# A 64-wide attention whose rotation takes one projection instead of two, with VectorE writing the sine products across blocks of 32 partitions

## The chip, the core and the metric

The kernel runs on one core of one Trainium2 chip. The metric is the device time of one execution in microseconds. Three runs of the kernel before gave 2931.18, 2931.95 and 2934.36 us. TensorE (PE) has two clock levels, 1.2 and 2.4 GHz; the profile states the granted clock as a share of the higher one. VectorE is DVE, ScalarE is ACT, GpSimd is POOL and SyncE is SP in the views.

## What is computed

The reference is a small hybrid network of two layers; the change touches only its first attention, `L0_attn_a`. Input x is 2 batches of 1024 tokens with 128 channels, layer-normalized before it comes in.

```python
NQ, NKV, HD, RANK = 16, 4, 64, 8          # 16 query heads share 4 key/value heads
def _lora_proj(x, W, A, Bm):
    return x @ W.T + x @ A.T @ Bm.T * LORA_SCALE
def _rope(x, cos_h, sin_h):
    x1, x2 = (x[..., ::2], x[..., 1::2])
    return jnp.concatenate([x1 * cos_h - x2 * sin_h, x1 * sin_h + x2 * cos_h], axis=-1)
q, k = _rope(q, cos_h, sin_h), _rope(k, cos_h, sin_h)
attn = jax.nn.softmax(jnp.einsum('bhqd,bhkd->bhqk', q, k) * ATTN_SCALE, axis=-1)
out = jnp.einsum('bhqk,bhkd->bhqd', attn, v)
return _lora_proj(out, Wo, qA..., oA, oB)
```

There is no mask: each of 16 heads x 2 batches has 1024 x 1024 scores.

## The kernel before, in words

`attention_l0a` loads the weights of the first key/value group and the tables, then `wide_heads` runs the whole attention in one block in which every engine has its own written-out order. The work is cut into `WINDOWS` = 8 windows (group g = w // 2, batch b = w % 2), and each window into `STEPS` = 32 steps; a step is one head's 128 query rows against all 1024 keys. So there are 256 steps, and in each:

- TensorE (L906 on) multiplies the scores of step s (L917, L918: four matmuls against the high and low parts of k), turns eight 128 x 128 blocks of finished rows of step t = s - 10 (L932), in every second step multiplies two such pieces with V (L944), and last does one of the jobs that `wide_jobs` placed in this step (`spare`).
- VectorE takes the row maximum of the scores (L1025), copies half of the turned blocks (L1031), takes the reciprocal of the sums of step s - 1 (L1037), writes low parts (`low`, L993) and reads the job's result (`read`).
- ScalarE copies the other half of the turned blocks (L967), takes the exponential with the row sum (L972), once in eight steps copies the head output (L977), divides the row of step s - 2 if `on_act` says so (L981), and writes high parts (`high`, L956 and L958).
- GpSimd adds cosine and sine products (L1056) and divides the other rows (L1059).

The turned blocks of a set of eight rows may start only when all eight rows are divided (L926, L927): transposes of a step s with s % 8 == 2 wait for the row of step s - 3. Scores wait for the exponential two steps back (L915), transposes for both copies of the step before (L930). GpSimd and VectorE go through their lists strictly in order, so a wait holds all that stands behind it.

A rotation unit ("rope") is one (window, u) with u from 0 to 5: u 0 and 1 are the two halves of k's 1024 tokens for a window, u 2 to 5 are two heads of q for one half each. Before the change, one unit is two jobs: f = 0 projects x with the columns in rotation order, f = 1 with the columns of each pair of halves swapped. VectorE multiplies the first by the cosine table into `t_cos`, the second by the signed sine table into `t_sin` (L1012), two buffers each. GpSimd adds them. ScalarE writes the rounded value once whole into `t_hi` and once into the stack (`Kh`, or the upper or lower 64 partitions of `Qw`), and VectorE writes the remainder, value minus rounded value, into the low stack (`Kl`, or the other 64 partitions of `Qw`). Scores of a window use the units made in the window before. The lead (step -1) does the first window's low-rank product and its units 0 to 2. Other jobs are "lora" (low-rank update of the weights of a group, L881 to L887), "value" (V of a window, L894) and "out" (the output projection, L902). All jobs share bank 7 of PSUM except those of the lead.

## Time and profile before

| | before |
|---|---|
| median of 3 runs | 2931.95 us |
| profiled execution, its time / its span | 2932.3 / 2930.6 us |
| PE matmul busy | 2285.7 us, 78% of the span |
| DVE / ACT / POOL busy | 1552.0 / 1456.3 / 903.7 us (53 / 50 / 31%) |
| mean granted TensorE clock | 0.876 |
| this attention | about 43 to 957 us of the span |

The shares hold for the whole program; the attention above takes the first third of it. In the page's line of 40 slices of 73 us, TensorE is at 9 tenths or more and at the full clock in slices 2 to 13, VectorE at 7, ScalarE at 6 to 7, GpSimd at 7. One reads such a profile by stretches: first which engine is full in the stretch, then its order of time, then what it waits for. Matmul ends are modelled, so the distance between starts says more than a single duration.

### The profile page before, as it was taken

The page shows a single profiled execution, that of the slowest core. Times are in us where ns is not written, and L with a number is a line of the kernel's source. Part 1 is how long each engine was busy: PE and PEld are TensorE (multiplying, and loading weights), DVE is VectorE, ACT ScalarE, POOL GpSimd, SP SyncE. Part 2 cuts the span into 40 slices and gives each one's busy share as a digit, 9 for nine tenths or more (in the row PEclk, how much of TensorE's full clock was granted, in tenths as well). Part 3 has the DMA queues.
Part 4 walks back from the last instruction along what each step waited for, and adds up shares of the span by engine and source line. Part 5 has one row for each costly group of instructions (what it writes and reads, how often), then busy time and mean ns, then how long its engine had stood idle before and what let it go on. Part 6 is the DMA issues. An engine that isn't in the chain of part 4 may idle for free. (4 is left out here: it accounts for less than half of the span.)

```text
span 2930.6 us, 38170 instructions
## 1 busy us (share of the span) xinstructions
PE 2285.7 (78%) x13956; PEld 1360.2 (46%) x13966; DVE 1552.0 (53%) x3280; ACT 1456.3 (50%) x2248; POOL 903.7 (31%) x512
## 2 busy tenths in 40 slices
PE   3999999999999339499428485899869515999788
PEld 2566666666665218333317343344347313344366
DVE  3767777777764351411351363677523395677323
ACT  2666666666675422488432244355633312555532
POOL 3776776777774102422201303100010122000100
PEclk9999999999999559699659798799979755999889
DMA  2000000000000300321300121211000002210000
GB/s 67 8 1 1 3 8 1 3 8 1 3 1 1 119 0 1 84 57 33 119 0 1 51 69 40 63 43 34 2 15 22 0 0 55 64 41 18 1 22 29
DMA packets 41593, 79.77 MB, mean 27 GB/s; under 512 B 11448, under 2 KB 20200, under 8 KB 37256
## 3 DMA queue, kind: packets, MB, share of 16 engines
q1 hardware_dynamic: 41416, 77.43, 9.7%
q8 instruction: 108, 1.77, 0.2%
q14 instruction: 69, 0.57, 0.1%
HBM read 63.03 MB, written 13.63 MB: 26 GB/s over the span
## 5 line engine op out<-in xcount | busy, mean ns | idle before, releaser
L648 ACT ACTIVATE probs<-psum_banks 128x1024 f32<-128x1024 f32 (+3 forms) x608 | 474.2, 826 | 360.3 <-PE psum_banks L513 253.1
L1059 POOL TENSOR_SCALAR l0a_rows<-l0a_rows,l0a_rinv 128x1024 f32<-128x1024 f32 x192 | 562.3, 2935 | 251.8 <-DVE l0a_rinv L1037 251.5
L721 DVE TENSOR_REDUCE neg_max<-psum_banks 128x1 f32<-128x512 f32 (+3 forms) x672 | 398.8, 658 | 201.1 <-PE psum_banks L546 149.5
L1025 DVE TENSOR_REDUCE l0a_nmax<-psum_banks 128x1 f32<-128x1024 f32 x256 | 312.9, 1222 | 208.1 <-PE psum_banks L918 207.4
L508 PE MATMUL psum_banks<-q_stack,k_stack 75*128 75x512 bf16 (+7 forms) x1216 | 322.7, 344 | 74.7 <-ACT probs L648 25.9
L972 ACT ACTIVATE l0a_rows<-psum_banks,l0a_nmax 128x1024 f32<-128x1024 f32 x256 | 285.9, 1117 | 79.8 <-DVE l0a_nmax L1025 77.5
L542 PE MATMUL psum_banks<-k_stack,q_stack 72*128 72x128 bf16 (+3 forms) x1024 | 250.7, 328 | 77.7 <-DMA q_stack<-q_parts 66.1
L932 PE MATMUL psum_banks<-packed,l0a_rows 128*128 128x128 f32 x2048 | 268.9, 274 | 7.8 <-POOL l0a_rows L1059 6.3
L932 PEld LDWEIGHTS psum_banks<-packed,l0a_rows 128*128 128x128 f32 x2048 | 238.8, 141 | 52.5 <-POOL l0a_rows L1059 11.5
L917 PE MATMUL psum_banks<-l0a_kh,l0a_qw 128*128 128x512 f32 x512 | 256.5, 501 | 6.2 <-DVE l0a_qw L993 5.9
L530 PE MATMUL psum_banks<-probs,v_ones 128*32 128x512 f32 (+3 forms) x2432 | 242.5, 514 | 7.5 <-ACT o_sum L617 6.5
L334 POOL TENSOR_SCALAR x_norm<-x_res,ln_mv,ln_rstd 128x128 f32<-128x128 f32 x128 | 101.4, 806 | 442.9 <-DVE ln_rstd L312 442.9
L508 PEld LDWEIGHTS psum_banks<-q_stack,k_stack 75*128 75x128 bf16 (+1 forms) x1216 | 105.5, 100 | 252.5 <-ACT probs L648 102.8
L918 PE MATMUL psum_banks<-l0a_kl,l0a_qw 128*128 128x512 f32 x512 | 204.9, 400 | 0.0
L334 POOL TENSOR_SCALAR x_norm<-l1f_y,ln_mv,ln_rstd 128x128 f32<-128x128 f32 x32 | 24.9, 792 | 540.1 <-DVE ln_rstd L312 540.1
L542 PEld LDWEIGHTS psum_banks<-k_stack,q_stack 72*128 72x128 bf16 x1024 | 95.7, 105 | 201.6 <-DVE neg_max L721 90.3
L1555 DVE SCALAR_TENSOR_TENSOR l1f_y<-psum_banks,rt_g,l1f_y 128x128 f32<-128x128 f32 x256 | 72.2, 345 | 168.3 <-PE psum_banks L1533 168.1
L917 PEld LDWEIGHTS psum_banks<-l0a_kh,l0a_qw 128*128 128x128 f32 x512 | 97.4, 190 | 134.9 <-issue 79.2
L967 ACT ACTIVATE x_norm<-psum_banks 128x512 f32<-128x512 f32 x128 | 75.9, 593 | 138.7 <-PE psum_banks L932 138.5
L1523 PE MATMUL psum_banks<-x_norm_t,l1f_w 128*128 128x512 f32 x256 | 117.2, 618 | 23.3 <-PEq L69 14.1
L513 PE MATMUL psum_banks<-tri_k,ident_b 128*128 128x128 bf16 (+1 forms) x566 | 127.9, 243 | 0.0
L944 PE MATMUL psum_banks<-x_norm,l0a_v 128*64 128x512 f32 x512 | 124.0, 604 | 3.7 <-ACT l0a_ot L977 3.7
(259 smaller groups left out, 3596.5 us busy)
## 6 DMA issues: line engine op xcount, KB each, us to landing
q_stack<-q_parts SPq DMA_DIRECT2D x96, 192.0 KB
k_stack<-k_parts SPq DMA_DIRECT2D x72, 192.0 KB
qkv<-in_l0f_w SPq DMA_DIRECT2D x6, 1024.0 KB, 5.5
q_parts<-parts SPq DMA_DIRECT2D x24, 256.0 KB
k_parts<-parts SPq DMA_DIRECT2D x24, 256.0 KB
l1f_w<-in_l1f_w SPq DMA_DIRECT2D x20, 256.0 KB, 2.9
moe_w<-in_l0f_w SPq DMA_DIRECT2D x2, 1024.0 KB, 5.5
packed<-in_packed SPq DMA_DIRECT2D x1, 1875.5 KB
```

The costliest lines, as they stand in the source:

```text
L508: m = pe.matmul(PS[:, bank, c0:HALF], S.Kst[0:rows_of_stack, slot(g, i), kt * P:(kt + 1) * P], S.Qst[0:rows_of_stack, slot(g, i), side * H ...
L513: m = pe.matmul(PS[:, bank, c0:c1], S.ident_b[:], S.tri_k[:, 0:c1 - c0], start=False, stop=True, skip_group_check=True)
L530: m = pe.matmul(PS[32 * i:32 * (i + 1), 7, c0:HALF], S.Vx[:, NT * b + kt, h0 + i, :], S.Pt[:, U % PBUFS, i, c0:HALF], start=kt == 0, stop= ...
L542: return pe.matmul(bank[:, at:at + k1 - k0], S.Qst[0:72, slot(g, i), jq * P:(jq + 1) * P], S.Kst[0:72, slot(g, i), k0:k1], start=first, st ...
L648: act.activation(S.Pt[:, U % PBUFS, 2 * half:2 * half + 2, c0:HALF], PS[:, bank:bank + 2, c0:HALF], ACT.Exp).then_inc(exp_done, 1)
L721: dve.tensor_reduce(out, scores, AX, ALU.max, negate=True).then_inc(job_read, 1)
L917: pe.matmul(scores(s)[:, c0:c0 + HALF], q, R.Kh[:, b, c0:c0 + HALF], start=True, stop=False)
L918: m = pe.matmul(scores(s)[:, c0:c0 + HALF], q, R.Kl[:, b, c0:c0 + HALF], start=False, stop=True)
L932: m = pe.transpose(PS[:, 4 + a, jj * P:(jj + 1) * P], R.Pr[:, (NT * ps + 2 * jj + a) % RING, kt * P:(kt + 1) * P], S.ident[:])
L972: act.activation(R.Pr[:, s % RING, :], scores(s), ACT.Exp, bias=R.nmax4[:, s % 4:s % 4 + 1], accum_out=R.rsum4[:, s % 4:s % 4 + 1]).then_i ...
L1025: dve.tensor_reduce(R.nmax4[:, s % 4:s % 4 + 1], scores(s), AX, ALU.max, negate=True).then_inc(max_done, 1)
L1059: pool.tensor_scalar(R.Pr[:, s % RING, :], R.Pr[:, s % RING, :], R.rinv4[:, s % 4:s % 4 + 1], None, ALU.mult).then_inc(pool_normed, 1)
```

## The change

One projection per unit. The swapped columns are gone from the weights: 448 columns per group instead of 896, and the sine table's signs are exchanged. VectorE multiplies the projection by the cosine as before, and then writes the sine product in four parts: part i reads partitions 32i to 32i + 31 of the projection and of the table, and writes to the neighbouring block of 32. Parts 0 and 1 come in the job's step, parts 2 and 3 at the job's place in the next step, after its reciprocal. The scale of q is in these multiplies. GpSimd's sum comes one step after the job, and now GpSimd also writes the low parts, three steps after it, subtracting the high part in its stack; VectorE's `low` and ScalarE's whole copy `t_hi` are gone. ScalarE writes the high parts three steps after the job. Rows divided on ScalarE are those with s % 8 in (1, 4, 6) instead of s % 4 == 1, that is 96 instead of 64 of 256. `wide_jobs` places the units at steps 1, 5, 9, 11, 19 and 21 of a window, those of window 1 at 9, 11, 13, 15, 17 and 19 of window 0. VectorE's cosine multiply of a unit waits until the high and low parts of the unit two before are done.

```diff
-    rope = [[("rope", w, u, f) for u in range(6) for f in range(2)] for w in range(WINDOWS)]
-    total, at = WINDOWS * STEPS, {-1: [("lora", 0, 0), ("lora", 0, 1)] + rope[0][:6]}
...
+    rope = [[("rope", w, u) for u in range(6)] for w in range(WINDOWS)]
+    total, at = WINDOWS * STEPS, {-1: [("lora", 0, 0)] + rope[0][:3]}
...
+            jobs = {1: rope[0][3], 3: rope[0][4], 5: ("value", 0), 7: rope[0][5], 21: ("value", 1), 23: ("lora", 0, 1)}
+            jobs.update(zip(range(9, 21, 2), rope[1]))
         else:
...
+            jobs = {15: ("out", w - 1, 0), 17: ("out", w - 1, 1)}
+            if not last:
+                jobs[13] = ("value", w + 1)
+                jobs.update(zip((1, 5, 9, 11, 19, 21), rope[w + 1]))
+        if w % 2 and g:
+            jobs[3] = ("lora", g, 1)
+        if w % 2 == 0 and g + 1 < NKV:
+            jobs[31] = ("lora", g + 1, 0)
...
+        sums_at.setdefault(s + 1 if s >= 0 else s, []).append(n)
+        highs_at.setdefault(s + 3 if s >= 0 else s, []).append(n)
+        lows_at.setdefault(s + 3 if s >= 0 else s, []).append(n)
...
     def on_act(s):
 
-        return s % 4 == 1
+        return s % 8 in (1, 4, 6)
...
                     if part == 0:
-                        m = pe.matmul(PS[:, bank, :], R.la[:, 0, :], R.lb[:, 0:512], start=True, stop=True)
-                    elif part == 1:
-                        pe.matmul(PS[:, bank, 0:256], R.la[:, 1, :], R.lb[:, 512:768], start=True, stop=True)
-                        m = pe.matmul(PS[:, bank, 256:384], R.la[:, 2, :], R.lb[:, 768:896], start=True, stop=True)
+                        for i, (c0, c1) in enumerate(((0, 256), (256, 384), (384, 448))):
+                            m = pe.matmul(PS[:, bank, c0:c1], R.la[:, i, :], R.lb[:, c0:c1], start=True, stop=True)
...
             def high(u):
-                scale, parts = targets(u)
                 act.wait_ge(summed, u + 1)
-                act.activation(R.t_hi[:, u % 2, :], R.t_cos[:, u % 2, :], ACT.Copy, scale=scale).then_inc(hi_done, 1)
-                for ch, hi, lo in parts:
-                    ins = act.activation(hi, R.t_cos[ch, u % 2, :], ACT.Copy, scale=scale)
-                ins.then_inc(copied, 1)
+                for rows, hi, lo in targets(u):
+                    ins = act.activation(hi, R.t_cos[rows, u % 2, :], ACT.Copy)
+                ins.then_inc(hi_done, 1)
...
-            def low(u):
-                scale, parts = targets(u)
-                dve.wait_ge(hi_done, u + 1)
-                dve.wait_ge(copied, u + 1)
-                for ch, hi, lo in parts:
-                    ins = dve.scalar_tensor_tensor(lo, R.t_cos[ch, u % 2, :], scale, R.t_hi[ch, u % 2, :].bitcast(F32),
-                                                   ALU.mult, ALU.subtract)
-                ins.then_inc(lo_done, 1)
+            def turn_part(job, blocks):
+
+                u = unit_no[job[1:]]
+                for i in blocks:
+                    src, to = slice(32 * i, 32 * i + 32), slice(32 * (i ^ 1), 32 * (i ^ 1) + 32)
+                    ins = dve.scalar_tensor_tensor(R.t_sin[to, u % 2, :], PS[src, bank_of(job), :], scale_of(job),
+                                                   R.sinT[src, job[2] % 2 * HALF:(job[2] % 2 + 1) * HALF], ALU.mult, ALU.mult)
+                return ins
...
                     if u >= 2:
-                        dve.wait_ge(lo_done, u - 1)
-                    table, to = ((R.cosT, R.t_cos), (R.sinT, R.t_sin))[f]
-                    ins = dve.tensor_tensor(to[:, u % 2, :], PS[:, bank, :], table[:, k % 2 * HALF:(k % 2 + 1) * HALF], ALU.mult)
+                        dve.wait_ge(hi_done, u - 1)
+                        dve.wait_ge(lo_done, low_parts(u - 2))
+                    dve.scalar_tensor_tensor(R.t_cos[:, u % 2, :], PS[:, bank, :], scale_of(job),
+                                             R.cosT[:, job[2] % 2 * HALF:(job[2] % 2 + 1) * HALF], ALU.mult, ALU.mult)
+                    turn_part(job, (0, 1))
+                    return
...
+                for job in at.get(s - 1, ()) if s > 0 else ():
+                    if job[0] == "rope":
+                        turn_part(job, (2, 3)).then_inc(job_read, 1)
...
+            def low(u):
+
+                pool.wait_ge(hi_done, u + 1)
+                for rows, hi, lo in targets(u):
+                    for own in (sums, rows_divided, lows):
+                        if own.n:
+                            own.wait()
+                    lows.link(pool.tensor_tensor(lo, R.t_cos[rows, u % 2, :], hi.bitcast(F32), ALU.subtract))
+
             for s in range(-1, total):
                 for u in sums_at.get(s, ()):
...
+                    total_of(u)
+                    if s < 0:
+                        low(u)
+                for u in lows_at.get(s, ()) if s >= 0 else ():
+                    low(u)
                 if s >= 0 and not on_act(s):
                     pool.wait_ge(inv_done, s + 1)
```

## Rows read from the trace of the kernel before

**Rows 1.** Stretches: us, busy us of PE, PEld, DVE, ACT, POOL, clock, DMA.

```profile
61.00:94.00 33.00, 26.61 (x91) 18.29 (x92) 23.29 (x33) 19.04 (x32) 24.57 (x10) 0.81 0.00 1
...
153.00:920.00 767.00, 759.89 (x4154) 487.25 (x4155) 549.32 (x848) 523.05 (x868) 547.48 (x208) 1.00 0.01 3
```

**Rows 2.** TensorE in order of time, two steps with a job: start, us, instruction.

```profile
302.47 0.50 PE L917 MATMUL psum_banks<-l0a_kh,l0a_qw 128*128 128x512 f32 x1
...
309.02 0.50 PE L917 MATMUL psum_banks<-l0a_kh,l0a_qw 128*128 128x512 f32 x1
```

**Rows 3.** TensorE in order of time, two steps without a job.

```profile
865.08 0.50 PE L917 MATMUL psum_banks<-l0a_kh,l0a_qw 128*128 128x512 f32 x1
...
870.74 0.50 PE L917 MATMUL psum_banks<-l0a_kh,l0a_qw 128*128 128x512 f32 x1
```

**Rows 4.** Waits from 94 to 920 us: total us, times, longest.

```profile
PE psum_banks L932 <- POOL l0a_rows L1059: 4.1, 10, 1.0
...
PE psum_banks L944 <- ACT l0a_ot L977: 3.7, 8, 0.5
```

**Rows 5.** Groups of VectorE, 42 to 960 us: busy us, mean ns; idle before.

```profile
L1025 DVE TENSOR_REDUCE l0a_nmax<-psum_banks 128x1 f32<-128x1024 f32 x256 | 312.9, 1222 | 208.1 <-PE psum_banks L918 207.4
...
L1031 DVE COPY x_norm<-psum_banks 128x512 f32<-128x512 f32 x128 | 87.3, 682 | 11.7 <-PE psum_banks L932 11.2
...
L1037 DVE RECIPROCAL l0a_rinv<-l0a_rsum 128x1 f32<-128x1 f32 x256 | 39.3, 153 | 0.2
...
L993 DVE SCALAR_TENSOR_TENSOR l0a_qw<-l0a_tc,l0a_ts 64x512 fp32r<-64x512 f32 x64 | 66.5, 1039 | 5.2 <-ACT l0a_qw L958 3.9
```

**Rows 6.** VectorE in order of time: a pair on changing partitions, then two neighbours.

```profile
59.82 1.39 DVE L993 SCALAR_TENSOR_TENSOR l0a_qw<-l0a_tc,l0a_ts 64x512 fp32r<-64x512 f32 x2 [1.38 <-ACT l0a_qw L958]
...
98.63 0.69 DVE L1012 TENSOR_TENSOR l0a_tc<-psum_banks,l0a_cos 128x512 f32<-128x512 f32 x1
...
99.23 1.21 DVE L1025 TENSOR_REDUCE l0a_nmax<-psum_banks 128x1 f32<-128x1024 f32 x1
```

**Rows 7.** Groups of ScalarE, 42 to 960 us, same columns.

```profile
L972 ACT ACTIVATE l0a_rows<-psum_banks,l0a_nmax 128x1024 f32<-128x1024 f32 x256 | 285.9, 1117 | 79.8 <-DVE l0a_nmax L1025 77.5
...
L972 ACT ACTIVATION_READ_ACCUMULATOR l0a_rows<-psum_banks,l0a_nmax 128x1 f32 x256 | 49.9, 195 | 0.0
...
L967 ACT ACTIVATE x_norm<-psum_banks 128x512 f32<-128x512 f32 x128 | 75.9, 593 | 138.7 <-PE psum_banks L932 138.5
...
L981 ACT ACTIVATE l0a_rows<-l0a_rows,l0a_rinv 128x1024 f32<-128x1024 f32 x64 | 73.2, 1143 | 0.0
...
L958 ACT ACTIVATE l0a_qw<-l0a_tc 64x512 fp32r<-64x512 f32 x64 | 39.9, 623 | 0.4
```

**Rows 8.** Single lines: instruction, count, ns min/median/max, first and last start.

```profile
L1056 POOL TENSOR_TENSOR l0a_tc<-l0a_tc,l0a_ts x48: 1263/1284/1777, 51.9 to 810.2; 128x512 f32<-128x512 f32 x48
...
L1059 POOL TENSOR_SCALAR l0a_rows<-l0a_rows,l0a_rinv x192: 2836/2845/3343, 66.7 to 927.3; 128x1024 f32<-128x1024 f32 x192
...
L993 DVE SCALAR_TENSOR_TENSOR l0a_qw<-l0a_tc,l0a_ts x64: 684/689/1762, 59.8 to 820.5; 64x512 fp32r<-64x512 f32 x64
```

**Rows 9.** All engines in order of time, around the lead.

```profile
45.42 0.69 DVE L1005 SCALAR_TENSOR_TENSOR l0a_w<-psum_banks,l0a_w 128x512 f32<-128x512 f32 x1 [21.94 <-PE psum_banks L881]
...
61.36 0.77 PE L917 MATMUL psum_banks<-l0a_kh,l0a_qw 128*128 128x512 f32 x1 [5.94 <-DVE l0a_qw L993]
```

**Rows 10.** TensorE in order of time, window 0, idle before in brackets.

```profile
79.25 1.31 PE L890 MATMUL psum_banks<-x_norm_t,l0a_w 128*128 128x512 f32 x2 [3.58 <-DVE l0a_tc L1012]
...
94.47 1.91 PE L932 MATMUL psum_banks<-packed,l0a_rows 128*128 128x128 f32 x8
...
152.85 1.09 PE L932 MATMUL psum_banks<-packed,l0a_rows 128*128 128x128 f32 x8 [1.03 <-POOL l0a_rows L1059]
```

**Rows 11.** DMA from 20 to 60 us: the queue (packets, MB), one transfer (KB).

```profile
q1 hardware_dynamic: 640, 1.69, 13.9%
...
l0a_w<-in_l0a_w SPq DMA_DIRECT2D x1, 448.0 KB
```

More of the change, by code:

```diff
@@ L808, in wide_heads @@
     lead = len(at[-1])
-    units = [job[1:3] for job in order if job[0] == "rope" and job[3] == 1]
+    units = [job[1:3] for job in order if job[0] == "rope"]
     unit_no = {u: n for n, u in enumerate(units)}
-    done_at = [step_of["rope", *u, 1] for u in units]
+    done_at = [step_of["rope", *u] for u in units]
     sums_at, highs_at, lows_at = {}, {}, {}
     for n, s in enumerate(done_at):
-        sums_at.setdefault(s, []).append(n)
-        highs_at.setdefault(s + 2 if s >= 0 else s, []).append(n)
-        next_use = step_of["rope", *units[n + 2], 0] if n + 2 < len(units) else total
-        lows_at.setdefault(min(s + 4, next_use) if s >= 0 else s, []).append(n)
+        sums_at.setdefault(s + 1 if s >= 0 else s, []).append(n)
+        highs_at.setdefault(s + 3 if s >= 0 else s, []).append(n)
+        lows_at.setdefault(s + 3 if s >= 0 else s, []).append(n)
     def item(s):
@@ L888, in spare @@
                 elif job[0] == "rope":
-                    pe.wait_ge(job_read, number["lora", job[1] // B, 1] + 1)
+                    pe.wait_ge(job_read, number["lora", job[1] // B, 0] + 1)
                     m = pe.matmul(PS[:, bank, :], columns(job), x[:, job[1] % B, job[2] % 2 * HALF:(job[2] % 2 + 1) * HALF],
@@ L893, in spare @@
                     for k in range(NT):
-                        m = pe.matmul(PS[:, bank, k * HD:(k + 1) * HD], x[:, job[1] % B, k * P:(k + 1) * P], R.W[:, 768:832],
+                        m = pe.matmul(PS[:, bank, k * HD:(k + 1) * HD], x[:, job[1] % B, k * P:(k + 1) * P], R.W[:, 384:448],
                                       start=True, stop=True)
@@ L911, in _ @@
                         u = unit_no[s // STEPS, 2 + s % STEPS // NT]
[L912 to L913 removed]
+                        pe.wait_ge(hi_done, u + 1)
+                        pe.wait_ge(lo_done, low_parts(u))
                     if s >= 2:
@@ L1037, in _ @@
                     dve.reciprocal(R.rinv4[:, r % 4:r % 4 + 1], R.rsum4[:, r % 4:r % 4 + 1]).then_inc(inv_done, 1)
-                if s < 0:
-                    for job in at[s]:
-                        if job[0] == "rope" and job[3] == 0 and unit_no[job[1:3]] >= 2:
-                            low(unit_no[job[1:3]] - 2)
-                        read(job)
-                    for u in lows_at[s][-2:]:
-                        low(u)
-                else:
-                    for u in lows_at.get(s, ()):
-                        low(u)
-                    for job in at.get(s, ()):
-                        read(job)
+                for job in at.get(s - 1, ()) if s > 0 else ():
+                    if job[0] == "rope":
+                        turn_part(job, (2, 3)).then_inc(job_read, 1)
@@ L1051, in _, with total_of @@
+                for job in at.get(s, ()):
+                    read(job)
+                    if s < 0 and job[0] == "rope":
+                        turn_part(job, (2, 3)).then_inc(job_read, 1)
         @block.gpsimd
         def _(pool):
+            sums, rows_divided, lows = Chain(pool, summed), Chain(pool, pool_normed), Chain(pool, lo_done)
+            def total_of(u):
+                pool.wait_ge(job_read, number["rope", *units[u]] + 1)
+                sums.mark(pool.tensor_tensor(R.t_cos[:, u % 2, :], R.t_cos[:, u % 2, :], R.t_sin[:, u % 2, :], ALU.add))
@@ L1737, in layouts @@
     half = np.concatenate([np.arange(0, HD, 2), np.arange(1, HD, 2)])
-    swap = np.concatenate([half[HD // 2:], half[:HD // 2]])
     cols = []
     for g in range(NKV):
-        q, k, v = [], [], []
-        for pair in range(2):
-            h0 = g * REP + 2 * pair
-            for order in (half, swap):
-                q += [h0 * HD + order, (h0 + 1) * HD + order]
-        for order in (half, swap):
-            k += [g * HD + order] * 2
-        v = [g * HD + np.arange(HD)] * 2
-        cols.append((np.concatenate(q), np.concatenate(k), np.concatenate(v)))
+        q = [(g * REP + h) * HD + half for h in range(REP)]
+        cols.append((np.concatenate(q), np.concatenate([g * HD + half] * 2), g * HD + np.arange(HD)))
     def per_group(q, k, v):
```

64 lines of the change are left out of this document (25 added, 39 removed).

## The prediction

> **What bounds the kernel now.** I read the stretches first. From 153 to 920 us, where seven of the eight windows of the first attention lie, TensorE is busy 99% of the time at a granted clock of 1.00; VectorE, ScalarE and GpSimd are at 72, 68 and 71% [rows 1]. The reader should see one full engine and three with a quarter left. The second view is TensorE's order of time. Two steps with one rotation job (scores, eight transposes, job, scores, eight transposes, the product with V) take 309.02 - 302.47 = 6.55 us, two without a job 870.74 - 865.08 = 5.66 us [rows 2, 3]. A rotation projection thus costs 0.89 us of the pace. The third view is the waits: TensorE's idle time on GpSimd's divided rows is 4.1 us in 10 places and 3.7 us in 8 on the copy of the head output [rows 4]. So in those windows TensorE's own work is the pace, and what is taken from it counts, as long as no other engine becomes late.
>
> **The sum starts from** the profiled execution, 2932.3 us for a span of 2930.6; 1.7 us lie around it, and it stands 0.35 us above the median of the runs, 2931.95. Nothing outside this stage is edited, so I leave the rest alone.
>
> **TensorE's work.** Each window's 12 projections become 6: 6 x 0.89 = 5.3 us. The low-rank product shrinks from 896 to 448 columns per group. A rotation's 512 columns cost 0.89, so this is 0.78 per group, 0.4 per window: 5.7 us per window. Work for windows 1 to 6 plus their share is removed; window 7 has no rotation job.
>
> **VectorE.** A unit loses one multiply, and its low part (one operation for k, two for q); it gains four sine parts on 32 partitions each. What does one part cost? Two neighbours on the same partitions follow at 99.23 - 98.63 = 0.60 although each lasts 0.69; a pair of L993 that changes partitions halfway took 1.39, so 0.70 each [rows 6]. The parts change partitions every time, so I take 0.70 and keep 0.60 as the low end; the high end is L993's mean beside GpSimd, 1.04 [rows 5]. In the Trainium skill, "VectorE: DVE Perf Modes", section "Two Vector instructions with no wait between them", an instruction whose input or output starts in another group of 32 partitions than its predecessor's begins only once everything earlier is finished; by it every part and the reduce behind it pay the full length.
> A unit then takes cosine 0.7 + 4 x 0.7 = 3.5 us, in two steps, beside 2 x 1.9 for reduce, copy and reciprocal (1.15 + 0.6 + 0.15, [rows 5] less the overlap): 7.3 us against TensorE's 6.55 for the same two steps. One rotation is absorbed; two in neighbouring odd steps, as at 9/11 and 19/21, are not.
> I walk steps 19 to 24 from the start of scores 19, with each engine in its order. TensorE alone would begin transposes 24 at 15.8. VectorE begins reduce 19 at 1.25, runs three rotation blocks (2.1, 1.4, 2.1) and three times 1.9, and reaches reduce 22 at 12.6. The exponential starts 1.26 later, lasts 1.2 with its accumulator, then ScalarE divides row 20 (1.15), writes the high parts of the unit of step 19 (2 x 0.62) and only then copies transposes 23 (0.6) [rows 7]: 18.05. TensorE needs that bank for transposes 24: 2.25 us late (1.2 if parts follow at 0.60). The same pair of jobs, divide and high parts, returns in step 24, and row 23 on GpSimd comes behind row 21, a sum and two low parts: 0.7 us more at step 26. At 9/11 TensorE waits only 0.25 us for a VectorE copy, since the value and output jobs of steps 13 and 15 give slack (eight matmuls with weights of their own, each at a quarter of 0.89: 1.8 us). Before, by the code's step numbers, the high parts met no divide in half of the windows, and a job in nearly every second step gave slack.
> ScalarE in total: 48 full high parts go (48 x 0.62 = 30 us), 32 divides come (32 x 1.14 = 37 us); its share hardly moves, its place does.
>
> **GpSimd.** 32 rows leave (32 x 2.84 = 91 us), 16 + 64 low parts come. Nothing shows a subtract on 64 partitions there; the sum of 128 x 512, 1.28 us [rows 8], is nearest, with the same 512 elements in a partition: 80 x 1.28 = 103 us. Bounds: 0.7 (half, if partitions counted) and 1.8, the longest L1056. In windows 1 to 7 the row before a transposed set of eight (row 6) moves to ScalarE, so row 7 starts at once; I give back the waits on rows, 0.7 us per window (4.1 us in [rows 4], and what follows late behind them), and four times 0.4 = 1.7 in window 7. Against it: without a job in step 3 or 27 the product with V waits for the copy of the head output, about 0.5 us in seven more places, 0.6 per window.
> L1059's times run from 2836 to 3343 ns and L993's from 684 to 1762 [rows 8], the long ones side by side; both go, as VectorE no longer has an operation with two SBUF inputs. In the Trainium skill, "SBUF — State Buffer", section "SBUF: two separate sides", only such operations (or the fast modes) take the port pair that GpSimd uses, so the sine parts should leave its rows at 2.84; the trace agrees, as L1012 reads PSUM and one table and lasts 0.69 beside it [rows 6].
>
> Per window: -5.7 + 2.25 + 0.7 + 0.25 + 0.6 - 0.7 = -2.6; six windows: -15.6. Window 7: -1.7.
>
> **The lead.** Now: low-rank read at 45.42, first scores at 61.36 [rows 9]. After: the shorter product and a single read let the first projection start about 1.5 us earlier, at 45.8; its cosine follows 2.1 later, as now; five operations per unit: units finished at 51.4, 54.9, 58.4. Behind the last: sum 1.28, two high parts 1.25, two low parts 2.6 on GpSimd, with hand-overs 63.7: +2.4. The load moves 448 KB less 224 [rows 11] of 1.69 MB, an eighth of a landing of 6 to 10 us: -0.7 (0 to -1.3).
>
> **Window 0.** Here units follow every two steps from 9 to 19, and VectorE's cosine of unit n waits for the low part of unit n-2 on GpSimd, two steps back. GpSimd has the row, the next unit's sum and that low part ahead: cosine and two parts 2.1, next reduce, copy, reciprocal 1.9, row 2.84, sum 1.28, low 1.3 or 2.6: 9.4 to 10.7 us per two steps where TensorE wants 6.55. Behind VectorE's wait stand the next reduce, and so exponential and scores. I followed this queue by the same prices: the cosines of window 1's units 1 to 5 may start 38.8, 48.4, 58.0, 69.0 and 78.5 us after scores 0, and then rows 18, 19, 21 and 23, a sum and two pairs of low parts bring GpSimd to 97.8, which frees transposes 26. Before, they came at 152.85 - 61.36 = 91.5, having waited 1.03 for GpSimd too [rows 9, 10]: +6.3. In that, the first ten steps gain: first transposes at 30.4 instead of 94.47 - 61.36 = 33.1. Behind it the low-rank job of step 31 is 0.9 shorter.
>
> **Sum:** -15.6 - 1.7 + 2.4 - 0.7 + 6.3 - 0.9 = -10.2: 2932.3 - 10.2 = 2922.1, less 0.35 to stand to the median: about 2922. What is late next is ScalarE's copy in steps 22 to 24, not TensorE.
>
> **Rivals.** *Full relief.* If the parts overlap (0.60) and slack swallows the rest, a window saves 5.7 + 0.7 - 1.0: six give -32; with the lead +1.7, window 0 at +1 and window 7: -31, 2901. For it: the three engines have a quarter free. Against: the walk above, with little freedom in it. *The clock.* In window 0 TensorE would idle a third of the time. Before, the stretch 61 to 94, with an idle of 3.58 us in it, stood at 0.81, so at 1.2 GHz in part [rows 1, 10]. If window 0 falls there for some ten steps (3.2 us of work doubles against a pace of 5.0), it costs 1.4 each, up to 14, central 7: 2929. Against: that stretch was 81% busy with gaps and still mostly at 2.4 GHz. *Slower: dear parts.* If a 32-partition part costs 1.04 like L993 beside GpSimd, each is 0.34 dearer. Six lie ahead of exponential 22 (+2.0), six ahead of step 12 (+1.5 beyond the slack), the two other blocks +0.5: +4.0 per window, +24, window 0's loop +4, the lead +4: 2922 + 32 = 2954. It turns from gain to loss at about 0.1 us per part above my price, 0.80. Against: no second SBUF input. A milder form, GpSimd's low part at 1.8, adds 0.5 x 12 in window 0 and 2 x 0.5 per window: +12, 2934. That the change doesn't do what it says can't be: the projections are gone from the code.
>
> **How the numbers follow.** Forecast 2914 to 2927: 0.42. Full relief: 0.24. Clock, or both small losses, 2927 to 2937: 0.20. Slower by dear parts or low parts: 0.14. The range leaves 0.1 beyond each end: 2899 to 2940. A measurement of this kernel tells 0.2%, 5.9 us, from no change: faster means below 2926.1, slower above 2937.8. Faster: nearly all of the forecast and the relief, 0.63; within: 0.24; slower: 0.13.
>
> **What would show it.** Right: projections 96 instead of 192 records; two neighbouring steps without job at 5.66, with one 6.55; sine parts of 0.69 that follow at 0.70; TensorE waiting on the ScalarE copy once or twice per window by about 2 us; VectorE cosine waiting on GpSimd in window 0; scores 0 near 63. Wrong: TensorE still 99% busy in windows 1 to 6, a granted clock below 1.00 there, GpSimd low parts far from 1.28, window 0 shorter than before.

## The result, and the profile after

The changed kernel takes 2941.93 us (median of 6 runs, 2939.27 to 2945.15) against 2930.86 for the kernel before (6 runs, 2927.70 to 2934.36): ratio 1.0039, 95% interval 1.0026 to 1.0051. It is slower by 11 us, where 2922 was predicted with a range of 2899 to 2940; slower had a chance of 0.13 there. The profiled execution took 2940.4 us for a span of 2938.3.

To see where the time went, I cut the stage at the start of the exponential of each window's first step. All lengths are us from the traces; 0-10, 10-26 and 26-32 are the steps within window 0.

```
              exp 0   w0     w1     w2     w3     w4     w5     w6     w7    | 0-10  10-26  26-32
before        64.7   109.5  109.6  107.7  110.3  108.6  110.3  107.5   95.6  | 31.4   58.3   19.9
changed       65.3   120.3  108.3  109.5  108.3  109.5  108.3  108.3   95.0  | 32.0   69.5   18.8
```

Window 0 is 10.8 us longer, the six steady windows together are only 1.7 shorter, window 7 is 0.6 shorter and the start 0.6 later. That is +9.1; what lies outside this stage gave 1.0 back.

The same two stretches as in [rows 1], now of the changed kernel (columns: stretch, its length, busy us of PE, PEld, DVE, ACT, POOL, granted clock, DMA):

```profile
61.00:94.00 33.00, 22.67 (x65) 14.90 (x66) 24.38 (x36) 17.13 (x26) 21.96 (x12) 0.76 0.00 0
153.00:920.00 767.00, 736.71 (x4102) 477.23 (x4101) 573.18 (x896) 540.36 (x863) 533.51 (x244) 1.00 0.01 2
```

TensorE was busy for 759.89 of 767 us before and now for 736.71. So its work did fall, but nearly all of what was taken away came back as idle time, at the full clock. VectorE rose from 549 to 573 us. TensorE's waits from 94 to 920 us, answering to [rows 4] (what waits, for whom: total us, times, longest):

```profile
PE psum_banks L935 <- ACT x_norm L968: 9.4, 6, 1.6
PE psum_banks L947 <- ACT l0a_ot L978: 7.6, 18, 0.6
PE psum_banks L935 <- DVE x_norm L1034: 7.3, 12, 1.9
PE psum_banks L935 <- POOL l0a_rows L1075: 5.0, 6, 0.8
PE psum_banks L893 <- DVE l0a_ts L994: 3.8, 5, 1.0
PE psum_banks L935 <- DVE l0a_cols L1034: 3.8, 2, 1.9
PE psum_banks L897 <- DVE l0a_ts L994: 3.4, 7, 0.5
```

Before there were two entries above 1.0 us, on GpSimd's rows and the head output. Now every engine holds TensorE somewhere. L994 are the sine parts: the projection (L893) and the value job (L897) wait for them because they free the one spare bank. The prediction had no such wait.

The prices of the single operations came out as forecast (groups over 61 to 920 us; busy us, mean ns | idle before):

```profile
L994 DVE SCALAR_TENSOR_TENSOR l0a_ts<-psum_banks,l0a_sin 32x512 f32<-32x512 f32 x180 | 123.6, 687 | 3.2
L1064 POOL TENSOR_TENSOR l0a_qw<-l0a_tc,l0a_qw 64x512 fp32r<-64x512 f32 x63 | 80.1, 1271 | 11.2 <-POOL l0a_qw L1064 5.2 <-POOL l0a_rows L1075 3.1 <-ACT l0a_qw L959 0.4
```

Four parts in a row took 2.79 us in the lead, 0.70 each. The low part on GpSimd costs 1.27 on 64 partitions.

### The profile page after: what moved, and what is told of

Its sections match the earlier page's. It is cut to its first block and busy times, and to the rows that moved or that the text cites. A ratio compares the mean times of both kernels' runs of the same rounds, so it can differ in the third digit from the quotient of the medians.

```text
span 2938.3 us, 38125 instructions
## 1 busy us (share of the span) xinstructions
PE 2247.8 (77%) x13860; PEld 1344.8 (46%) x13870; DVE 1582.7 (54%) x3340; ACT 1469.2 (50%) x2232; POOL 896.6 (31%) x560
## 3 DMA queue, kind: packets, MB, share of 16 engines
q8 instruction: 107, 1.75, 0.2%
## 5 line engine op out<-in xcount | busy, mean ns | idle before, releaser
L1075 POOL TENSOR_SCALAR l0a_rows<-l0a_rows,l0a_rinv 128x1024 f32<-128x1024 f32 x160 | 454.9, 2845 | 221.6 <-DVE l0a_rinv L1040 218.6
L935 PE MATMUL psum_banks<-packed,l0a_rows 128*128 128x128 f32 x2048 | 272.1, 275 | 27.6 <-ACT x_norm L968 10.1
L920 PE MATMUL psum_banks<-l0a_kh,l0a_qw 128*128 128x512 f32 x512 | 244.8, 478 | 17.1 <-POOL l0a_qw L1064 13.8
L994 DVE SCALAR_TENSOR_TENSOR l0a_ts<-psum_banks,l0a_sin 32x512 f32<-32x512 f32 x192 | 131.9, 687 | 3.4
L229 PE MATMUL psum_banks<-packed,x_norm 128*128 128x128 f32 x160 | 38.2, 385 | 118.2 <-POOL x_norm L334 118.2
```

The lines of the kernel that those rows point to most:

```text
L920: pe.matmul(scores(s)[:, c0:c0 + HALF], q, R.Kh[:, b, c0:c0 + HALF], start=True, stop=False)
L935: m = pe.transpose(PS[:, 4 + a, jj * P:(jj + 1) * P], R.Pr[:, (NT * ps + 2 * jj + a) % RING, kt * P:(kt + 1) * P], S.ident[:])
L994: ins = dve.scalar_tensor_tensor(R.t_sin[to, u % 2, :], PS[src, bank_of(job), :], scale_of(job), R.sinT[src, job[2] % 2 * HALF:(job[2] % 2 ...
L1075: rows_divided.mark(pool.tensor_scalar(R.Pr[:, s % RING, :], R.Pr[:, s % RING, :], R.rinv4[:, s % 4:s % 4 + 1], None, ALU.mult))
```

## Where a steady window's time goes

TensorE in order of time, window 3 of the changed kernel, the instructions with an idle time before them (in brackets, with its releaser):

```profile
428.84 0.66 PE L935 MATMUL psum_banks<-packed,l0a_rows 128*128 128x128 f32 x4 [0.49 <-DVE x_norm L1034]
...
447.41 2.00 PE L897 MATMUL psum_banks<-l0a_w,x_norm_t 128*128 128x64 f32 x16 [0.48 <-DVE l0a_ts L994]
...
485.94 1.09 PE L935 MATMUL psum_banks<-packed,l0a_rows 128*128 128x128 f32 x8 [1.55 <-ACT x_norm L968]
...
492.66 1.09 PE L935 MATMUL psum_banks<-packed,l0a_rows 128*128 128x128 f32 x8 [0.84 <-POOL l0a_rows L1075]
...
499.89 1.94 PE L947 MATMUL psum_banks<-x_norm,l0a_v 128*64 128x512 f32 x8 [0.47 <-ACT l0a_ot L978]
```

Measured against the shortest distance between starts of the same kind, these and a few small ones lose 0.71, 0.70, 1.75, 0.99 and 0.53 us, with 0.43 and 0.21 for two more head-output copies, 0.25 at step 12 and 0.24 at step 22: 5.8 in all. The windows are not alike, before least of all (107.5 to 110.3 us, by the jobs in them), so the comparison has to be over all six. Windows 1, 2, 4 and 6 of the changed kernel lose another 0.9 in step 4, where a VectorE copy is late as well as the head output. By the same reckoning (all differences above 0.06 us), a window had 107.8 us of TensorE's work and 1.2 of stalls before, and has 102.1 and 6.6 now. The work fell by 5.7, the stalls rose by 5.4.

The largest wait is on a ScalarE copy. VectorE and ScalarE in order of time ahead of it show who is late first:

```profile
476.59 1.23 DVE L1028 TENSOR_REDUCE l0a_nmax<-psum_banks 128x1 f32<-128x1024 f32 x1
477.73 0.68 DVE L1034 COPY l0a_cols<-psum_banks 128x512 f32<-128x512 f32 x1
478.45 0.16 DVE L1040 RECIPROCAL l0a_rinv<-l0a_rsum 128x1 f32<-128x1 f32 x1
478.53 0.67 DVE L1012 SCALAR_TENSOR_TENSOR l0a_tc<-psum_banks,l0a_cos 128x512 f32<-128x512 f32 x1
479.21 1.38 DVE L994 SCALAR_TENSOR_TENSOR l0a_ts<-psum_banks,l0a_sin 32x512 f32<-32x512 f32 x2
480.60 1.23 DVE L1028 TENSOR_REDUCE l0a_nmax<-psum_banks 128x1 f32<-128x1024 f32 x1
...
482.65 1.40 DVE L994 SCALAR_TENSOR_TENSOR l0a_ts<-psum_banks,l0a_sin 32x512 f32<-32x512 f32 x2
484.08 1.22 DVE L1028 TENSOR_REDUCE l0a_nmax<-psum_banks 128x1 f32<-128x1024 f32 x1
```

```profile
481.86 1.12 ACT L973 ACTIVATE l0a_rows<-psum_banks,l0a_nmax 128x1024 f32<-128x1024 f32 x1 [2.12 <-DVE l0a_nmax L1028]
482.87 0.19 ACT L973 ACTIVATION_READ_ACCUMULATOR l0a_rows<-psum_banks,l0a_nmax 128x1 f32 x1
482.97 1.14 ACT L982 ACTIVATE l0a_rows<-l0a_rows,l0a_rinv 128x1024 f32<-128x1024 f32 x1
484.01 1.25 ACT L959 ACTIVATE l0a_qw<-l0a_tc 64x512 fp32r<-64x512 f32 x2
485.28 0.60 ACT L968 ACTIVATE x_norm<-psum_banks 128x512 f32<-128x512 f32 x1
```

VectorE has no idle time here (the copy and the reciprocal behind the second reduce are left out), and from the reduce at 476.59 to that two steps later at 484.08 it needs 7.49 us where TensorE wants 6.55 [rows 2]. ScalarE stood idle for 2.12 us because the maximum was late, and then ran exponential, row, two high parts and the copy in series.

## The experiments

Each kernel was timed against runs of the kernel before on the same chip. "Windows 1 to 6" is the mean of the six; it is 109.0 before and 108.7 after the change. e4_one_sine and e9_two_parts leave out the exchange of 32-partition blocks that the rotation needs, so they measure time only. The diffs are shortened to what changes.

```
                        time (ratio, 95%)                windows 1-6 | 0-10  10-26  26-32
before                                                      109.0    | 31.4   58.3   19.9
changed                 2941.9  1.0039 (1.0026-1.0051)      108.7    | 32.0   69.5   18.8
e1_cos_ring4            2931.1  0.9996 (0.9987-1.0006)      108.7    | 32.1   57.3   19.1
e2_parts_in_step        2956.5  1.0079 (1.0062-1.0096)      110.2    | 30.9   74.1   19.1
e3_high_later           2955.2  1.0079 (1.0062-1.0095)      110.1    | 30.1   69.5   18.8
e4_one_sine             2900.8  0.9894 (0.9872-0.9917)      104.1    | 26.0   62.6   18.9
e5_spread               2937.0  1.0020 (1.0008-1.0032)      107.6    | 32.0   69.5   18.8
e6_exchange             2899.1  0.9901 (0.9884-0.9917)      104.2    | 26.9   57.8   19.1
e7_low_vector           2993.9  1.0215 (1.0198-1.0232)      115.9    | 36.8   69.0   18.8
e8_before_act           2926.8  0.9987 (0.9978-0.9997)      108.1    | 33.5   57.8   19.4
e9_two_parts            2903.3  0.9909 (0.9892-0.9925)      104.4    | 26.6   64.5   19.0
e10_exchange_spread     2896.8  0.9884 (0.9867-0.9900)      103.7    | 27.0   57.9   19.1
e11_exchange_rows       2950.3  1.0070 (1.0054-1.0087)      110.5    | 30.8   65.8   18.8
e12_low_vector_later    2956.2  1.0088 (1.0068-1.0108)      110.6    | 35.0   70.5   19.1
```

**The waiting loop of window 0.** VectorE in order of time in window 0 of the changed kernel: the cosine waits for the low part of the unit two before.

```profile
113.71 0.69 DVE L1012 SCALAR_TENSOR_TENSOR l0a_tc<-psum_banks,l0a_cos 128x512 f32<-128x512 f32 x1 [2.25 <-POOL l0a_kl L1064]
...
123.63 0.69 DVE L1012 SCALAR_TENSOR_TENSOR l0a_tc<-psum_banks,l0a_cos 128x512 f32<-128x512 f32 x1 [2.32 <-POOL l0a_kl L1064]
...
134.97 0.69 DVE L1012 SCALAR_TENSOR_TENSOR l0a_tc<-psum_banks,l0a_cos 128x512 f32<-128x512 f32 x1 [3.75 <-POOL l0a_qw L1064]
```

The five cosines of window 1's units 1 to 5 follow at 9.8, 9.9, 11.3 and 9.9 us. The experiment opens the loop:

```diff
-R.t_cos[:, u % 2, :]            # two buffers
+R.t_cos[:, u % 4, :]            # four; waits: sum of u-2, high and low of u-4
```

> The cosine product gets four buffers, so VectorE's cosine of unit n waits for the low part of unit n-4 and for the sum of unit n-2 only. The theory of the waiting loop (VectorE waits for GpSimd's low part two units back, GpSimd's row waits for VectorE's reciprocal): window 0, 120.3 us in the changed kernel, falls to 108 to 113, windows 1 to 6 stay at 108 to 110 each, the whole is 8 to 12 us shorter than the changed kernel, about 2932. The theory of the held bank (a projection may start only after parts 2 and 3 of the one before, one step later, and scores stand behind it): window 0 stays above 117, about 2940.

Steps 10 to 26 fell from 69.5 to 57.3 us, 1 below the kernel before, and the steady windows didn't move. The loop is the whole of window 0's loss, and with it gone the change is worth nothing: 2931.1 against 2931.4. With the loop open, VectorE's own list is the pace. Its cosines now follow at 7.49 us without a gap, where TensorE wants 6.55:

```profile
101.57 0.67 DVE L1014 SCALAR_TENSOR_TENSOR l0a_tc<-psum_banks,l0a_cos 128x512 f32<-128x512 f32 x1
...
109.06 0.67 DVE L1014 SCALAR_TENSOR_TENSOR l0a_tc<-psum_banks,l0a_cos 128x512 f32<-128x512 f32 x1
```

The clock took part too. Steps 10 to 26, first of the changed kernel, then of this one (columns as in [rows 1]):

```profile
97.00:167.00 70.00, 59.45 (x279) 36.87 (x279) 51.36 (x79) 41.98 (x68) 51.33 (x29) 0.88 0.02 4
97.00:155.00 58.00, 51.84 (x277) 32.49 (x277) 51.07 (x79) 41.90 (x68) 51.61 (x29) 1.00 0.02 5
```

In the loop TensorE waited again and again, and for 17 of some 70 us it stood at 1.2 GHz; with the loop open it stayed at 2.4. Of the 12.2 us gained, 4.4 are less idle time and 7.8 are the same work done in less time.

**The held bank.** Parts 2 and 3 come a step after the job, and the bank is held until then.

```diff
-turn_part(job, (0, 1))          # (2, 3) after the next step's reciprocal
+turn_part(job, (0, 1, 2, 3))    # all in the job's step
```

> All four sine parts are written in the job's own step, none in the next, so bank 7 is free before the next job. Theory of the held bank: the waits of TensorE's jobs on sine parts (about 0.7 us per window at step 13, 3.0 and 2.6 us in the first ten steps) go, windows 1 to 6 each about 1 us shorter and window 0 by 5 or more: about 2931 in all. Rival, the next reduce comes 1.4 us later and costs more than the bank gave: windows 1 to 6 each 1 to 4 us longer, 2945 to 2960. Theory of the waiting loop: window 0 keeps its period of 9.9 us per two steps.

This is the rival's branch: the next reduce came late. The first ten steps gained 1.1 us, no more than that stretch differs by between executions of the same code (below, e3_high_later). Each steady window grew by 1.5, and steps 10 to 26 by 4.6. The loop did not keep its period, which rose to between 10.1 and 12.7 us. Four parts in one step put that step's successor late. Two parts per step is the better place for them, and the bank is the smaller part of the matter.

**ScalarE's high parts.** If the copy at transposes 24 is late because a row and two high parts stand ahead of it, moving the high parts one step should help.

```diff
-highs_at, lows_at: s + 3
+highs_at, lows_at: s + 4        # for jobs of windows 1 to 6
```

> From window 1 on, high and low parts come four steps after the job instead of three, so no high part shares a ScalarE step with a divide. Theory that the ScalarE step with both is what takes the steady windows' gain: the wait of 1.75 us at transposes 24 and most of the 1.0 at transposes 26 go, windows 1 to 6 each 2 to 2.7 us shorter: about 2942 - 14 = 2928. Theory that VectorE's load sets them: TensorE then waits elsewhere for VectorE, windows stay within 0.7 us of 108.3 and 109.5: 2938 to 2942.

Both expectations were missed: the windows grew to 110.1. TensorE's waits in window 3 of this kernel (403 to 512 us), and GpSimd in order of time:

```profile
PE psum_banks L935 <- POOL l0a_rows L1075: 2.1, 1, 2.1
PE psum_banks L935 <- DVE x_norm L1034: 1.1, 2, 0.7
...
PE psum_banks L935 <- ACT x_norm L968: 0.3, 1, 0.3
```

```profile
489.30 1.28 POOL L1064 TENSOR_TENSOR l0a_qw<-l0a_tc,l0a_qw 64x512 fp32r<-64x512 f32 x1 [0.97 <-ACT l0a_qw L959]
490.74 1.28 POOL L1064 TENSOR_TENSOR l0a_qw<-l0a_tc,l0a_qw 64x512 fp32r<-64x512 f32 x1 [0.17 <-POOL l0a_qw L1064]
492.12 5.67 POOL L1075 TENSOR_SCALAR l0a_rows<-l0a_rows,l0a_rinv 128x1024 f32<-128x1024 f32 x2
```

The wait on ScalarE fell from 1.6 to 0.3 as meant, but the low parts moved with the high parts and now stand ahead of two rows, so the wait on GpSimd's row rose from 0.8 to 2.1. That is the exchange of one wait for another in window 3, which rose by 0.8. Windows 1 and 5 rose by 2.4 and 2.5, and there the clock is the difference: behind the same wait of 2.1 us the granted clock is 0.69 from 275 to 280 us, and 0.66 from 715 to 720, where window 3 has none of it. A product with V that otherwise takes 1.87 us to the next scores took 3.33. Windows 0 to 6 explain 6 of the 13 us by which the median lies above the changed kernel's; the profiled execution was the shortest of the four, at 2949.8. Steps 0 to 10 have the changed kernel's code here and took 30.1 us against 32.0: two executions can differ by 2 us in that stretch.

**VectorE's time.** One sine operation on 128 partitions in place of four on 32; the exchange of blocks is left out.

```diff
-for i in blocks: src, to = 32-partition block i, block i ^ 1    # two parts a step later
+src, to = all 128 partitions, the same                         # in the job's step, which frees the bank
```

> One sine multiply over 128 partitions in the job's step in place of the four parts; the exchange of neighbouring blocks is left out, so the attention's values differ. It shows what the four parts cost. Theory that VectorE's 2.1 us per unit are what delays the exponentials: windows 1 to 6 fall to about 103 to 104 each (work 102.1), window 0 by 10 or more: 2900 to 2906. Theory that ScalarE's order decides by itself: transposes 24 still wait over 1 us, windows 105 to 107: 2912 to 2925.

This is 41 us off the changed kernel, as the first theory had it. Steady windows fell to 104.1, the first ten steps from 32.0 to 26.0. TensorE's waits in window 3 are these and no others:

```profile
PE psum_banks L947 <- ACT l0a_ot L978: 0.9, 2, 0.5
PE psum_banks L935 <- POOL l0a_rows L1069: 0.7, 1, 0.7
```

The wait for ScalarE's copy is gone though ScalarE's list is unchanged: what was late was VectorE. How steep is it? Two parts on 64 partitions cost 1.4 us per unit, between 0.7 and 2.8:

```diff
-for i in (0, 1) / (2, 3): blocks of 32, i ^ 1
+for i in (0,) / (1,):     blocks of 64, i ^ 1
```

> The changed kernel with the sines written by two operations over 64 partitions, one in the job's step and one in the next, in place of four over 32; blocks of 64 change places instead of blocks of 32, so the rotation is not the reference's. Per unit VectorE has 1.4 us for the sines, between 0.7 of the one operation and 2.8 of the four. If the price of VectorE's time is even, windows 1 to 6 stand a third of the way between 104.1 and 108.7, at 105.6, the time at 2909 to 2918. If VectorE first fills idle time and only the last part is dear, they stand at 104 to 104.7 and the time at 2902 to 2908. Rival: the wait for the bank that is held until the next step, not VectorE's time, is what costs: then windows are as in the changed kernel, 108 or more, and the time is 2930 or more.

Windows of 104.4 and 2903.3 us: the second expectation. From 0.7 to 1.4 us per unit a window grew by 0.3, from 1.4 to 2.8 by 4.3. The measured pair above needs 7.49 us; by subtraction it is 6.1 with two parts and 5.4 with one. TensorE's pair takes 6.55. Below that the extra work is all but free, above it TensorE pays. The held bank is ruled out as the main cost, for this kernel holds it over the same step.

**Crowding.** Do units two steps apart make it worse?

```diff
-jobs.update(zip((1, 5, 9, 11, 19, 21), rope[w + 1]))
+jobs.update(zip((1, 5, 9, 19, 23, 27), rope[w + 1]))
```

> The changed kernel with the rope jobs of windows 1 to 6 at steps 1, 5, 9, 19, 23 and 27 in place of 1, 5, 9, 11, 19 and 21; window 0 is as it was. No operation is added or dropped. Crowding theory: a unit gives VectorE 3.5 us on top of 4.1 us for each pair of steps, 7.6 us where a pair of steps lasts some 6.5, so two units two steps apart put VectorE and behind it ScalarE's copies late (the 1.55 us at transposes 24). Spread, each window loses 1.5 to 3 us: windows 1 to 6 at 106 to 107.5, the time 2924 to 2933. Rival: the late copies follow the jobs to steps 20, 24 and 28, and the windows stay at 108 to 109.5, the time at 2939 to 2945.

Neither: 1.1 us per window, 2937.0, between the two. Every pair with a unit exceeds 6.55 by itself, so spreading stops the sum of two delays but not each one. Window 3 of this kernel shows it: TensorE is late three steps after each of the six units, by 0.43, 0.72, 1.34, 0.71, 0.84 and 0.73 us, and four of the six times it waits for a VectorE copy.

**Low parts back on VectorE**, the rest as changed:

```diff
-lows.link(pool.tensor_tensor(lo, R.t_cos[rows], hi.bitcast(F32), ALU.subtract))
+dve.scalar_tensor_tensor(lo, R.t_cos[rows], 1.0, hi.bitcast(F32), ALU.mult, ALU.subtract)
```

> The changed kernel with the low parts back on VectorE (in front of the step's job, three steps after the projection), all else as changed. By the price that one sine operation showed (12.6 us of VectorE taken from a window gave 4.6 us), 7 us of low parts per window cost 2.5 us, less the 0.8 us wait for GpSimd's row: windows 1 to 6 at 110 to 111; window 0 is shorter by 2 to 6 us, since the low part that its loop waits for is shorter. Time 2944 to 2956. Rival (GpSimd's low parts are the dear part of the change): windows 107 or less, time 2930 or less.

Each window grew by 7.2 us where 1.3 to 2.3 were expected, and window 0 is 4.3 longer where 2 to 6 less were expected. VectorE's low parts from 153 us on (busy, mean ns | idle before and who ended it):

```profile
L992 DVE SCALAR_TENSOR_TENSOR l0a_qw<-l0a_tc,l0a_qw 64x512 fp32r<-64x512 f32 x52 | 41.4, 796 | 46.1 <-ACT l0a_qw L959 45.3
...
L992 DVE SCALAR_TENSOR_TENSOR l0a_kl<-l0a_tc,l0a_kh 128x512 fp32r<-128x512 f32 x12 | 8.3, 692 | 26.2 <-ACT l0a_kh L959 26.2
```

VectorE stood for 71.5 us waiting for the high parts, which ScalarE writes at the end of the same step, with reduce and copy queued behind. One step later they are there:

```diff
-lows_at: s + 3
+lows_at: s + 4
```

> The changed kernel with the low parts on VectorE, four steps after the projection in place of three, so that ScalarE's high part is written by then and VectorE doesn't stand waiting for it (71.5 us from 153 us on in the kernel with three steps, some 10 us per window). If that wait was what made it 7.2 us per window slower, windows 1 to 6 stand at 108.7 to 110 and the time at 2935 to 2948. If it is the 7 us per window of work on VectorE, which a pair of steps with a unit can't hold (9.0 us against 6.55), they stand at 112 to 115 and the time at 2960 to 2985.

110.6, between the two branches: 5.3 of the 7.2 us were the wait, 1.9 the work. The 5.3 include a lower clock behind the waits: over windows 1 to 6 the granted clock is 0.97 in e7_low_vector, and 1.00 in the changed kernel and here. So the low parts' move to GpSimd is a gain of about 1.9 us per window, and not the fault of the change. In window 0 it is not shown: the first ten steps are 3 us longer than in the changed kernel, but that stretch varies by 2 by itself. The result also bounds the rule of the pair. Pairs with a unit and low parts were put at 9.0 us of VectorE's time, 1.5 above the changed kernel's, and the window grew by only 1.9 in all. VectorE catches up in the pairs without a unit, so what a pair has too much is a warning and not a price.

**Rows on ScalarE.** This part alone, on the kernel before:

```diff
-return s % 4 == 1
+return s % 8 in (1, 4, 6)
```

> The kernel before with 3 of 8 rows divided on ScalarE in place of 1 of 4, and nothing else. Forecast's step: the waits of 0.7 us for GpSimd's rows go, and ScalarE's added 4.6 us per window lie in idle time: 2925 to 2931. Rival: ScalarE's copies come late behind the added divisions, as at transposes 24 in the changed kernel, 1 to 2 us per window: 2936 to 2944.

2926.8, the forecast's branch; 0.9 us off a window. TensorE's waits from 94 to 920 us, beside [rows 4], show that it is the wait on GpSimd's rows:

```profile
PE psum_banks L944 <- ACT l0a_ot L977: 3.7, 8, 0.5
PE psum_banks L890 <- DVE l0a_tc L1012: 1.3, 2, 1.0
PE psum_banks L932 <- POOL l0a_rows L1059: 0.9, 1, 0.9
```

**A version that beats both.** VectorE writes the sine product in one operation to a buffer of its own, and four transfers exchange the blocks. SyncE's queue had only the weights of the next group to load there.

```diff
+dve.scalar_tensor_tensor(R.t_un[:], PS[:, bank, :], scale, R.sinT[...], ALU.mult, ALU.mult)
+# SyncE, for each unit, after the job is read and the sum of u-2 is done
+for i in range(4):
+    sp.dma_start(R.t_sin[32 * (i ^ 1):32 * (i ^ 1) + 32, u % 2, :],
+                 R.t_un[32 * i:32 * i + 32, :]).then_inc(swapped, 16)
-sums_at: s + 1     t_cos: 2 buffers
+sums_at: s + 2     t_cos: 3 buffers
```

> The changed kernel, but behind the lead each unit's sines are written by one operation over 128 partitions, unexchanged, and four transfers of 64 KB on SyncE's queue exchange the blocks of 32; the sum on GpSimd comes one step later, and the cosine has three buffers in place of two. Theory (VectorE's four part operations took the gain): windows 1 to 6 at 103.5 to 104.8 as with one sine operation, window 0 at 97 to 105, because three buffers open the waiting loop; the time is 2890 to 2902. Rival: transfer and its waits take longer than the two steps that they have, GpSimd then divides rows late behind the waiting sum, and windows stand at 107 or more, the time at 2920 or more.

2899.1 us, 1.0% below the kernel before, with windows of 104.2 and a window 0 of 103.8, all as the theory had it. The transfers, from the page's list of DMA issues (count, KB each, median us from issue to landing):

```profile
l0a_ts<-l0a_tu SPq DMA_DIRECT2D x180, 64.0 KB, 2.0
```

The median is 2.0 us and the longest 3.9. The Trainium skill, "DMA: Bandwidth & Descriptors", section "Anatomy of one DMA — SWDGE (gpsimd) path", gives a transfer issued from GpSimd a fixed cost of about 2.0 us, and its fit gives, as an estimate, 2.2 us for 64 KB. These transfers were issued from SyncE, for which that section has no figure, and took about as long. Spread over 1, 5, 9, 19, 23 and 27 as well:

> The kernel with the exchange by transfers, and rope jobs at steps 1, 5, 9, 19, 23 and 27 of windows 1 to 6. If VectorE is no longer crowded, spreading gives nothing: windows 1 to 6 at 103.5 to 104.8, the time at 2896 to 2901. If crowding still costs, windows lose another 0.5 to 1 us, the time is 2890 to 2895.

2896.8 us, the ratio 0.9884 (0.9867 to 0.9900): time and windows (103.7) lie in the first branch, though the windows are 0.5 us shorter than in e6_exchange, the least that the second had. In window 3 the only wait of TensorE left is the head output's:

```profile
PE psum_banks L959 <- ACT l0a_ot L990: 1.6, 3, 0.7
```

The time's own interval overlaps with that of e6_exchange, so only the windows show the difference. Last, the rows put back in e6_exchange, 1 of 4 on ScalarE:

> The kernel with the exchange by transfers, with 1 of 4 rows divided on ScalarE again in place of 3 of 8. GpSimd has 4 more divisions of 2.85 us per window, 11.4 us on top of some 75, beside low parts of 11 us. If those divisions matter with the low parts on GpSimd, the waits for its rows grow from 0.8 us to 2 to 5 us per window: the time is 2906 to 2925. Rival: idle time takes them, as GpSimd waits 25 us per window: 2896 to 2902.

2950.3: 6.3 us per window and 11.5 in window 0, more than the whole change costs, and beyond both expectations. TensorE's waits in window 3 of it, and GpSimd in order of time:

```profile
PE psum_banks L947 <- POOL l0a_rows L1094: 4.2, 3, 3.3
```

```profile
482.08 1.28 POOL L1083 TENSOR_TENSOR l0a_qw<-l0a_tc,l0a_qw 64x512 fp32r<-64x512 f32 x1 [0.17 <-POOL l0a_qw L1083]
483.46 2.84 POOL L1094 TENSOR_SCALAR l0a_rows<-l0a_rows,l0a_rinv 128x1024 f32<-128x1024 f32 x1
486.27 1.28 POOL L1074 TENSOR_TENSOR l0a_tc<-l0a_tc,l0a_ts 128x512 f32<-128x512 f32 x1
487.53 2.85 POOL L1094 TENSOR_SCALAR l0a_rows<-l0a_rows,l0a_rinv 128x1024 f32<-128x1024 f32 x1
490.61 1.26 POOL L1083 TENSOR_TENSOR l0a_qw<-l0a_tc,l0a_qw 64x512 fp32r<-64x512 f32 x1 [0.23 <-POOL l0a_rows L1094]
```

Between the rows a transposed set waits for stand sums and low parts. Here too the clock adds to it: over windows 1 to 6 (181 to 844 us) the granted clock is 0.98 against 1.00 in e6_exchange, and of the 6.3 us 3.8 are idle time of TensorE and 2.5 longer busy time. The same 32 rows are worth 0.9 us per window in the kernel before and 6.3 here. The two kernels differ in pace as well as in the low parts, so the 5.4 between them are not shown to be the low parts' alone; that the low parts stand in front of the row is.

## Why the prediction was wrong, point by point

The sum was -10.2 us; the profiled execution came out at 2940.4 - 2932.3 = +8.1, so 18.3 were missed: 13.8 in the stalls of windows 1 to 6 and 5.4 in window 0; window 7 (1.1), the lead (-1.1) and what lies outside the stage (-1.0) make up the rest.

- **TensorE's work** (-5.7 per window): measured -5.7.
- **Stalls per window** (+3.1 net: 2.25, 0.7, 0.25, 0.6 less 0.7): measured +5.4 as a mean of the six (109.0 - 5.7 + 5.4 = 108.7). This is the step that failed: 2.3 us in each of six windows. Single terms held: transposes 24 lost 1.75 for 2.25 (1.2 to 2.25 foreseen), step 26 lost 0.99 for 0.7, step 12 0.25 for 0.25. The head output's copies cost 1.2 in window 3, for 0.6. What was missing is a VectorE copy late at step 8 (0.71) and in four windows at step 4, the value job's wait for the held bank (0.70), and step 22 (0.24). I walked only the two crowded places and declared that a single rotation in a pair is absorbed, after having written 7.3 against 6.55 in the line before. It isn't: e9_two_parts at 6.1 us per pair stands at 104.4, the change at 7.49 at 108.7, and e5_spread, with single rotations only, still at 107.6.
- **Window 0's loop** (+9.0 for steps 10 to 26): the mechanism was right, and so was the period. The walk had the cosines 9.6, 9.6, 11.0 and 9.5 us apart, and they came 9.8, 9.9, 11.3 and 9.9 apart; the size was +11.2. e1_cos_ring4 shows it is this loop.
- **The clock** (a rival, +7, up to 14): window 0 did fall to 1.2 GHz in part, for 17 us of steps 10 to 26 against 1 before. But the loop's cosines are only 1.3 us further apart in all than the walk at full clock had them, so the price was not paid on top there. In windows 1 to 6 the clock stayed at 1.00, and the loss there has nothing to do with it.
- **The first ten steps** (-2.7): measured +0.6, transposes 0 at 95.12 - 61.97 = 33.1 us after scores 0, not 30.4. TensorE in order of time:

```profile
72.46 1.13 PE L893 MATMUL psum_banks<-x_norm_t,l0a_w 128*128 128x512 f32 x2 [3.00 <-DVE l0a_ts L994]
...
78.75 3.68 PE L897 MATMUL psum_banks<-l0a_w,x_norm_t 128*128 128x64 f32 x16 [2.59 <-DVE l0a_ts L994]
```

  The bank was held for the second pair of parts, and the value job then ran at a granted clock of 0.66 (76 to 86 us), in part at 1.2 GHz, 3.68 us long where it takes 2.00 at 447.41. Four parts against one explain 6.0 (e4_one_sine), the bank by itself at most 1.1 (e2_parts_in_step). The clock's own share was not set apart. Of the 6.0 us, 1.9 are less idle time of TensorE and 4.2 less busy time, with 12 us at 1.2 GHz in the changed kernel and 6 in e4_one_sine.
- **The lead** (+2.4 less 0.7): +0.6. Cosines at 45.81, 49.34 and 52.86 confirm 3.5 us per unit, but the units were finished 2.1 us before the working's times, of which the load was to give 0.7, and the tail behind them took 5.6 us for 5.3. **The last steps of window 0**: -1.1 for -0.9. **Window 7**: -0.6 for -1.7.
- **The prices**: 0.70 for a part, 1.28 for a low part, rows at 2.85: right. The rival "dear parts" had the wrong mechanism, though the loss that it named (VectorE ahead of the exponential) is where the time went. It wanted dearer parts; the number of parts was enough.
- **Two SBUF inputs.** With VectorE's low part gone, all 160 rows lasted 2841 to 2852 ns, where they went up to 3343 [rows 8]. In e7_low_vector, though, with such operations back on VectorE, they stayed at 2840 to 2856, and VectorE's low parts on 64 partitions were the longer ones (a mean of 796 ns from 153 us on). In e12_low_vector_later the rows had a mean of 2878 and went up to 3332. So the effect depends on what meets what. The L1012 that the prediction shows [rows 6] ran while GpSimd was idle; the point holds all the same, for 90 of the 96 L1012 ran beside a GpSimd operation, and none took more than 692 ns.

"Full relief" (2901, chance 0.24) is near what e4_one_sine and e6_exchange gave in total, though by other terms (4.9 us per window for 5.4, and a shorter window 0 for a longer one): the relief was real, and VectorE stood in its way.

## What to carry to other kernels

When work is taken off the full engine, the time per step falls, and every other engine has to fit the new, shorter period: add up each engine's list for the shortest stretch that repeats (here a pair of steps: 7.49 against 6.55 us), not its share of the span (72%). An operation on a quarter of the partitions costs as much as on all (0.69 us for 32, 0.68 for 128), so an exchange across partitions by parts multiplies the engine's time by their number; transfers can do it when the result isn't needed for a few microseconds. And before sending work to an in-order engine, look at which consumer's item it will stand in front of: putting the same 32 row divisions back cost 6.3 us per window in one kernel and 0.9 in another.

## What was not expected of the hardware

- VectorE's time shows a knee, not a slope: +0.3 us per window for the first 4.2 us added, +4.3 for the next 8.4.
- A wait can be paid twice. Behind waits of 2.1 us (e3_high_later, windows 1 and 5) and 3.3 us (e11_exchange_rows) TensorE was granted 1.2 GHz for some microseconds, and the matmuls behind the wait took up to twice as long. It is not regular: behind the same 2.1 us in window 3 of e3_high_later the clock stayed at 2.4 GHz.
- Four transfers of 64 KB per unit within SBUF, issued every two steps, landed in 2.0 us and disturbed nothing that can be seen: windows of 104.2 beside 104.1 without them.
- The rest of the program behind the last exponential took 2004.0 to 2013.4 us in the profiled executions, with no edit in it; differences of a few microseconds between single executions can come from there.
